# A hybrid layer on one core: waits between pairs of result fetches in GpSimd's queue

## The reference

```python
x = x + mamba(_layernorm(x))            # 128 heads of 64, state 128, 8 groups
x = x + ffn(_layernorm(x))
x = x + (_layernorm(x) @ (weight * mask).T)
x = x + ffn(_layernorm(x))              # the same weights a second time

def ffn(x2):
    gu_s = x2 @ shared_w_gate_up.T
    g_s, u_s = jnp.split(gu_s, 2, axis=-1)
    shared_out = jax.nn.silu(g_s) * u_s @ shared_w_down.T
    probs = jax.nn.softmax(x2 @ gate_w.T, axis=-1)
    topk_vals, topk_idx = jax.lax.top_k(probs, 2)      # 2 of 16 experts
    topk_vals = topk_vals / jnp.sum(topk_vals, axis=-1, keepdims=True)
    ...
    return moe_out + shared_out
```

## Time and profile before

| | us |
|---|---|
| median of 3 timed runs | 2003.55 (2002.83 to 2004.82) |
| profiled execution, its own time | 2019.41 |
| its span, first to last instruction | 2017.7 |
| PE busy | 1966.0 (97%) |
| DVE busy | 1468.4 (73%) |
| ACT busy | 1191.6 (59%) |
| POOL busy | 1031.9 (51%) |

### The profile page before, as it was taken

How to read it: one execution, slowest core, us unless ns; L and a number is a source line. 1 busy time by engine, 2 the same in 40 slices (tenths; PEclk the granted TensorE clock), 3 DMA queues, 4 the chain that set the end, 5 groups by cost and what they waited for, 6 DMA issues and landing times.

```text
span 2017.7 us, 38125 instructions
## 1 busy us (share of the span) xinstructions
PE 1966.0 (97%) x11776; PEld 1634.3 (81%) x11776; DVE 1468.4 (73%) x2764; ACT 1191.6 (59%) x2602; POOL 1031.9 (51%) x907
## 2 busy tenths in 40 slices
PE   5999999999999999999999999999999999989998
PEld 4888888888888888888888888888888878877886
DVE  7998499849975997599669866985798572177215
ACT  3786378538853884487449645964696435433441
POOL 1497059616951694179328922881398126240423
PEclk8999999999999999999999999999999999999999
DMA  2551135214512351234134312431353159932895
GB/s 92 165 169 57 44 120 171 61 37 125 161 52 64 112 156 43 87 109 136 43 92 129 112 43 93 148 102 33 98 161 93 33 178 354 333 95 74 325 371 159
DMA packets 143909, 253.92 MB, mean 126 GB/s; under 512 B 21448, under 2 KB 37832, under 8 KB 143696
## 3 DMA queue, kind: packets, MB, share of 16 engines
q1 hardware_dynamic: 134848, 231.35, 36.0%
q0 software_dynamic: 7520, 16.80, 2.7%
q10 hardware_dynamic: 1328, 3.15, 0.4%
HBM read 233.38 MB, written 25.69 MB: 128 GB/s over the span
## 4 chain that ended last, share of the span: by engine, by line
PE 89%; DVE 6%; issue 2%; ACT 1%; DMA 1%; another core or an unknown queue 1%; POOL 0%; DVEq 0%; ACTq 0%; SPq 0%; POOLq 0%
PE bank L1668 59%; PE bank L1787 7%; PE bank L1978 6%; PE bank L1801 5%; PE bank L1741 4%; PE bank L1990 3%; PE bank L1769 2%; DVE Y L1264 1%; PE bank L1965 1%; DVE spare L1361 1%; PE bank L1760 1%; PE bank L1808 1%; PE bank L1676 1%; DVE Y L1273 1%
## 5 line engine op out<-in xcount | busy, mean ns | idle before, releaser
L1668 PE MATMUL bank<-xh,wh 128*128 128x512 f32 x1288 | 523.9, 407 | 10.2 <-POOL wl L720 4.0
L1668 PE MATMUL bank<-xh,wl 128*128 128x512 f32 x1288 | 504.8, 392 | 0.0
L1668 PE MATMUL bank<-xl,wh 128*128 128x512 f32 x1288 | 503.0, 391 | 0.0
L720 POOL TENSOR_TENSOR wl<-raw,wh 128x512 fp32r<-128x512 f32 x144 | 192.6, 1342 | 462.6 <-ACT wh L877 462.6
L1264 DVE SCALAR_TENSOR_TENSOR Y<-bank,cpar,Y 128x511 f32<-128x511 f32 (+2 forms) x384 | 286.9, 747 | 23.5 <-ACT Y L921 14.3
L1668 PEld LDWEIGHTS bank<-xh,wh 128*128 128x128 f32 x1288 | 243.2, 189 | 60.5 <-POOL wl L720 4.9
L1668 PEld LDWEIGHTS bank<-xh,wl 128*128 128x128 f32 x1288 | 242.4, 188 | 54.1
L1668 PEld LDWEIGHTS bank<-xl,wh 128*128 128x128 f32 x1288 | 243.6, 189 | 45.7 <-issue 0.5
L737 POOL TENSOR_TENSOR Y<-Y,gt 128x512 f32<-128x512 f32 x128 | 183.6, 1434 | 94.5 <-DVE gt L1318 92.7
L1326 DVE TENSOR_TENSOR al<-Y,ah 128x512 fp32r<-128x512 f32 x128 | 95.9, 749 | 184.4 <-ACT ah L979 184.4
L1668 PE MATMUL bank<-wh,ah 128*128 128x512 f32 x544 | 213.6, 393 | 0.7
(11 more groups left out here) (231 smaller groups left out, 4033.8 us busy)
## 6 DMA issues: line engine op xcount, KB each, us to landing
mem<-c_rows SPq DMA_DIRECT2D x128, 256.0 KB, 3.8
mem<-wffn_d SPq DMA_DIRECT2D x62, 512.0 KB
E<-e_rows SPq DMA_DIRECT2D x256, 96.0 KB, 3.5
raw<-wconv_d SPq DMA_DIRECT2D x80, 256.0 KB, 2.9
cv<-c_rows SPq DMA_DIRECT2D x64, 256.0 KB, 4.0
spare<-c_rows SPq DMA_DIRECT2D x64, 256.0 KB, 4.1
raw<-wgate_d SPq DMA_DIRECT2D x64, 256.0 KB, 2.7
raw<-wout_d SPq DMA_DIRECT2D x64, 256.0 KB, 2.6
```

The lines of the kernel that those rows point to most:

```text
L720: inc(pool.tensor_tensor(wl[:, W_SLOT[p], :], raw[:, R_SLOT[p], :], wh[:, W_SLOT[p], :], ALU.subtract), w_lo)
L1668: got = mm(out, l, r, start=first and n == 0, stop=last and n == 2)
```

## The change

In front of each pair of fetches but the first, GpSimd gets one wait, for a step of the second shared product: pairs 1 to 7 wait for gate 1, gate 2, up 2, up 3, gate 4, up 4 and the second down step. Nothing else is edited; no instruction on another engine moves.

```diff
--- before.py
+++ after.py
@@ -790,6 +790,11 @@
                 for q in range(Y_RING):
                     pool.wait_ge(ty_out[q], 16 * uses(Y_RING, run, max(n for n in range(TILES) if n % Y_RING == q)))
                 for t in range(TT):
+                    if 1 <= t < TT - 1:
+                        unit_done, n = ((g_mm, 1), (g_mm, 2), (u_mm, 2), (u_mm, 3), (g_mm, 4), (u_mm, 4))[t - 1]
+                        now(pool, unit_done, second, n)
+                    elif t:
+                        now(pool, dn_mm, second, 2)
                     for c in range(2):
                         pool.indirect_dma_start(
                             back(c, t), None, slots_y,
```

## The result

| | before | changed |
|---|---|---|
| median of 20 runs each, us | 2004.36 (2002.18 to 2006.7) | 2008.89 (2005.81 to 2010.87) |
| ratio | | 1.0021, 95% interval 1.0015 to 1.0027 |
| profiled execution, us | 2019.41 | 2010.07 |
| its span, us | 2017.7 | 2008.3 |

The changed kernel is 4.5 us slower. The time lies above the range given, and on the side that had a chance of 0.08. At the same time its profile is 9.4 us shorter than the profile of before. Both need an explanation. Three of all the executions of this document took far longer than the others of their kernel (2203, 4148 and 6280 us); they are left out of every ratio and interval, but not of the medians given as measured.

A forecast was written before the change was run, and what follows sets the result against it. TensorE, busy 97% of the span, bounds the kernel, so GpSimd edits gain only where it stands still. 2003.55 + 0.7 = 2004.2 us, no measurable change; range 1991.5 to 2006.0 us.

The forecast's parts named there:

- the base of 2003.55 us: Timed median of the kernel before, taken as nearly free of late TensorE completions; the change's cost was added to it.
- +0.7 us: Cost of the waits over both feed-forward places, from VectorE getting pair 4 later; bounds +0.2 and +1.8 us.
- The lateness, 11.7 us: Up 3 and gate 4 seen late during GpSimd's fetch bursts, costing 5.2 and 6.5 us in the two places.
- the lateness belongs mostly to the profiled execution: Inferred from 2019.41 us profiled against 2003.55 us timed: timed runs see little of the 11.7 us; chance 0.54.
- The sign that was to confirm the forecast: Profiled time of the changed kernel falls, to 2010 us or less, while its timed median stays.
- Pairs 1 to 3 free: GpSimd's waits on gate 1, gate 2 and up 2 cost nothing, those steps having completed before the pairs are reached.
- Pair 4 issued 0.1 us behind up 3: GpSimd starts pair 4 0.1 us after TensorE's up 3, +2.1 us later than before; first place the same to 0.1 us.
- +0.35 us a place: VectorE's up multiply of step 4 moves +0.8 to +1.6 us, 0.7 us absorbed, leaving +0.1 to +0.9 a place.
- Pair 7 covered with 0.3 us to spare: Second place: pair 7 lands at 2003.9 us, before busy VectorE comes to it at about 2004.2 us.
- (A): Late completions are real in timed runs and the waits cure them: 1992.6 us; chance 0.32, including 0.06 for half cure.
- (B): Late completions are real but the waits don't cure them, fetches staying nearly as dense: 2004.6 us; chance 0.06.
- (C): Pairs land 3 us later, TensorE idling before its second four down steps, 3 us lost per place: 2010 us; chance 0.08.

The follow-up runs named there:

- e6: The changed kernel unchanged, run again at the low level: 2008.95 us, ratio 1.002 to the kernel before.
- e5: The kernel before unchanged, run again with its own profile at the low level: 2003.81 us, ratio 0.9995.
- e14: The kernel before unchanged, run and profiled at the high level: 2017.44 us, ratio 1.0007.
- e1: The changed kernel with only the wait before pair 4 (up 3) kept, the other six removed: 2008.95 us, ratio 0.9962 to the kernel before, high level.
- e3: The changed kernel with four waits only, pairs 4 to 7 on gate 3, up 3, gate 4, up 4: 2007.32 us, ratio 0.9955, high level.
- e13: The changed kernel unchanged, run at the high level: 2009.17 us, ratio 0.9968 to the kernel before.
- e9: The changed kernel with SyncE's output stores held back until all pairs are added: 2008.3 us, ratio 0.9979 to the kernel before, high level.
- e11: The changed kernel with only the wait before pair 7 (down 2) kept: 2010.26 us, ratio 0.9986 to the kernel before, high level.
- e7: The changed kernel with later waits, pairs 4 to 7 on gate 4, up 4, down 2, down 4: 2015.31 us, ratio 1.0049, low level.
- e15: The same edit as e3, run at the low level: 2004.76 us, ratio 0.9998 to the kernel before.
- e12: The same edit as e3, run again at the high level: 2006.36 us, ratio 0.9968 to the kernel before.
- e2: The changed kernel without the wait before pair 4, the other six kept: 2008.02 us, ratio 0.9957 to the kernel before, high level.
- e8: The kernel before with VectorE's adds of pair 4 moved behind low part 4 and pair 7's just ahead of the last down add: 2010.33 us, ratio 1.0024, low level.

## Why the prediction was wrong, step by step

The timed runs of the result stood at the low level, where there is no lateness, so the base of 2003.55 us was right for them. The time missed by the term added to it, +0.7 us, which measured 4.0 to 5.1 (e6 against the before of its job and against e5; 4.5 in the result). How the base was argued failed as well, but did not move the number; that comes first.

**The lateness, 11.7 us: size right, place wrong.** That up 3 and gate 4 were seen 3 to 7.5 us late, and that this cost about 11.7 us, held: the levels of the kernel before lie 8 to 14 us apart (2013.26 to 2017.44 against 2003.81 to 2004.95), in timed executions. (The traces give 10.7 us for e14 and 13.7 for the profile of before against e5, 7.1 and 6.6 by place, where the prediction had 5.2 and 6.5.) The step that failed is the one the prediction called its weakest, "the lateness belongs mostly to the profiled execution". It compared 2019.41 with 2003.55 us as a profile with its own timed runs. They stood at different levels: in e14 and e5 the profiled execution lies within 1.6 us of the median of its own job, at either level. That the base came out right all the same was luck: the timed runs happened to be at the low level. The thought that completions queue behind the records of the recorder is not settled; e5, which was recorded, has no lateness, so recording alone does not make it. What the prediction should have asked is whether three timed runs and one profile came from like conditions.

**The sign that was to confirm the forecast confirmed nothing.** "The profiled time falls while the median stays" was to confirm the forecast. The profile fell by 9.4 us as forecast, because its before was at the high level; the timed median did not stay but rose by 4.5 us at the low one.

**Pairs 1 to 3 free**: right, GpSimd's fetches stand at the earlier trace rows's spacing until pair 4. e1, with the wait of pair 4 alone, is at the changed kernel's time.

**Pair 4 issued 0.1 us behind up 3**: it was 0.8. Up 3 is due at 1971.88 - 0.06 + 5 x 2.72 = 1985.42 us, the fetch begins at 1986.21. Against ScalarE, whose tanh starts 5.44 us behind the last one, GpSimd starts 0.7 us later after its event. The 0.1 was assumed and rested on no row of GpSimd. (Up 3's time counts on the tanh starting 0.06 us behind its step, as the prediction took it. Without that: in e3 GpSimd starts 0.74 us behind ScalarE on the same gate 3.) Counted from the first tanh of its place, pair 4's first fetch goes 2.7 us later in e6 than in e5 and its second 2.65 us later, not 2.1. For the first place the prediction's own numbers give +1.8, not "the same to 0.1 us".

**+0.35 us a place**: the mis-sized term, by which the time missed. e5 against e6 gives +1.0 in the first and +3.0 in the second. The late restart of GpSimd (0.7 us) is as large as what the first place was short of (0.65). In the second place 0.85 us arises ahead of pair 7 (3.02 - 2.17), much as in the first, and 2.17 is the wait for pair 7.

**Pair 7 covered with 0.3 us to spare**: failed. It went 2.9 us late, and it landed after 5.1 to 5.7 us (e13, the changed kernel's profile, e6) instead of 3.7, beside the first output store, which was in no term of the sum. Where the prediction had 0.3 us to spare VectorE waited 2.17 us (e6). The stores are queued behind VectorE's down adds and not behind GpSimd, so a later pair is pushed into them (e9).

**Rivals.** (A), real and cured, 1992.6 us: the mechanism is right at the high level (e13, 0.9968) but its base was wrong, since the waits bring 2016 down to 2009 and do not take 2003.5 to 1992. At the low level there is nothing to cure. (B), real and not cured: refuted at the high level, three waits hold nothing back but the one before pair 4 is enough (e1), and without it most of the lateness returns (e11). (C), slower by pairs that land later: the direction and roughly the price (+4.5 for +6), but only in part the mechanism. It named as the point TensorE's down matmuls running out, 3 us in each place, for pairs that take 3 us longer to land. In the changed kernel pair 4 took 3.5 to 3.6 us to land, no longer than reckoned; it left late. TensorE did not idle before its second four down steps in either place (after, e6), so the sign that (C) asked for was absent too. Only its aside on pair 7 ("pair 7's 0.3 us is where it would begin") named what happened, in the second place. It had 0.08 because the earlier trace rows show landings in a stretch without stores. The Trainium skill (DMA: Bandwidth & Descriptors, "Rules for kernel authors") has the rule to issue a DMA early and wait late; at the low level the runs agree, 4.5 us lost (with e7's still later waits 10 us), at the high level the measurement goes the other way, 6.5 us gained (e13).

**What stays open.** What it is in a job that makes TensorE's completions late during back-to-back indirect fetches. e5 and e14 have the same program and the same fetches at 1.32 us, one without lateness and one with 7 us. The profile names no source, and no kernel here could set the level. That a pause in the burst keeps gate 4 on time is shown (e13 beside e14 in one job); the mechanism in between is not.

## What to carry to other kernels

Before a gap between a profile and timed runs is put down to the recorder, profile the same kernel once more beside runs taken with it: this kernel stood at two levels, and an edit that lost 4.5 us at one gained 6.5 at the other. A wait that paces one engine by another's progress should be hung on an event that is due just before the instruction would be reached anyway; then here it cost nothing where all was well (e15) and worked where it was needed (e3, e12). When a step is moved later, look not only at what waits for it but at which transfers it will now run beside.

## What the runs showed of the hardware

- The completions of TensorE's last matmuls, seen by ScalarE and VectorE, lagged by up to 7.6 us (e14) behind TensorE's own even pace while GpSimd issued 14 to 16 indirect fetches of 128 rows at 1.32 us. Gate 4 appeared 0.0 to 2.0 us after the end of the last of them, in six places of three traces (before, e14, e11). For gate 3, some eight fetches in, the lag was 0 to 2.9 us. It happened in three jobs and in the profile of before, and in no trace of the two jobs at the low level.
- GpSimd's indirect fetch begins 0.74 us after ScalarE's tanh where both wait for the same event (gate 3 in e3, 1776.12 against 1775.38; gate 4 in e7, 1991.58 against 1990.84).
- From the issue of a pair's second fetch of 128 rows of 2 KB to VectorE's start, where VectorE waited for it: 3.4 to 3.8 us for the first pair of the second place and for pair 4 of both, 4.1 to 5.6 for the first pair of the first place, where no output store runs, and 5.0 to 6.3 for pair 7 with an output store issued beside it (3.8 in e9, where the store was held back; 4.6 for pair 6 in e2).
- Behind a wait of TensorE of 3.07 us the granted clock was at the 1.2 GHz level (0.50 from 1808 to 1810 us) in e8, and the whole edit cost 6 us between the places, more than the wait itself.
